# A recurrent attention block with an MLP on one core: LoRA's products ahead, loads in another order, weight halves and one conv tap on ScalarE

## The chip, the cores and the metric

The kernel runs on one core of a Trainium2 chip. The metric is the device time of one execution in microseconds. The core has TensorE (PE, with its weight loads as PEld), VectorE (DVE), ScalarE (ACT), GpSimd (POOL) and SyncE (SP), each with an instruction queue of its own that is worked off in order. Engines wait for each other by semaphores. A "bank" is one of eight PSUM banks of 128 x 512 fp32.

## The reference

The input is x, 8 sequences of 512 tokens of width 128. Per sequence:

```
xn = layernorm(x)
z, xBC, dt = split(xn @ in_proj_w.T)            # 256, 384, 4 columns
dt = softplus(dt + dt_bias)
xBC = silu(conv_b + sum_k shift(xBC, k) * conv_w[:, k])      # 4 taps, causal
x_ssm, B, C = split(xBC)                        # 256, 64, 64; B and C are 32 complex numbers
theta = clip(theta_base + tanh(xn @ theta_w1) @ theta_w2, -pi/2, pi/2)      # LoRA, 4 heads x 32
log_z = complex(-(lambda_base + eta * theta**2) * dt, theta * dt)
state_t = exp(log_z_t) * state_{t-1} + B_t * (x_ssm_t * dt_t)      # per head, 64 x 32 complex
y_t = real(C_t . state_t) + D * x_ssm_t
g = rmsnorm(y * silu(z)) * norm_w
attention = g @ out_proj_w.T
h = 2*relu(s0 * [xn, -xn] @ (+-1)); h = 2*relu(s1 * h @ (+-1)); mlp = s2 * h @ (+-1)      # 512, 512, 128
out = x + attention + mlp
```

## The kernel before

One sequence is one turn of a software pipeline. Turn n holds the front of sequence n (theta, phases, decays, the MLP), the back of sequence n-1 (the products that give y, the gate, the output projection) and the first projections of sequence n+1. There is a prologue (weights made ready, first projections), a first turn without a back, six middle turns, a turn without a successor, and a drain that holds the last back alone. A general version follows for inputs whose exponents are large; a flag skips it, and it does not run here.

The order of the work on each engine is written out by hand: `pipelined(n, ...)` in each engine's block and `first_turn` on DVE and ACT. An instruction deep in one queue can hold up all behind it. The names that the change touches:

- **High and low halves.** fp32 values are multiplied as a high and a low fp16 half. For xn, `xn_t` makes xh on ACT and `xn_low` makes xl on DVE (L521). For weights, `pair` makes both on DVE (L923, L924) during the prologue. For the MLP, `mlp_high` makes h0h and h1h on ACT (L1132), `h0_low` and `h1_low` make h0l and h1l on DVE (L784); four tiles each.
- **Phases and decays (DVE).** `thetas` clips; `phases` multiplies theta with dt spread over the partitions in bank 2 (`ph`, L580), scans (L581), removes whole turns and leaves the fraction (L599). `exponents` multiplies rates with dt into `lz` in bank 2 (L607), scans it into SBUF (L613) and clamps it there (L614). ACT makes sine and cosine (`trig`, L1097 to L1100) and the growth factors by exp into bank 3 (`decays`, L1106 and L1114), with a table load ahead of the first exp. `decayed(n, 0)`, `(n, 1)` and `(n, 2)` multiply K, Q and U by them (L657), real and imaginary part in two instructions each.
- **B and C.** `bc_products` (PE, L1424) fills bank 2. `bc_taps` sums four taps on DVE: the newest one (L564), then three more (L567). `silu_bc` (ACT, L1071) and 16 DMAs on SP repeat the rows. POOL rotates C by the phases, waits for msq and makes `rms` (L1253), multiplies B with the rotated C (U, L1272 to L1277), and then makes B times K (L1302 to L1307, signal `s_bk`), which the products "across the middle" (PE, L1493) need.
- **LoRA.** `lora1` (PE, L1398) writes bank 3 and waits for the decay of U, which reads it; `tanh_lora` on ACT; `lora2` (PE, L1438) writes banks 3 and 1; `theta_input` on ACT (L1086). `dt_spread` (PE, L1445) transposes dt into bank 2 once the taps have been read.
- **The back.** PE makes G (L1483), across (L1493); DVE masks four heads (`g_base`, L715); PE transposes K (L1503), makes y within a chunk (L1513, L1520), the states (L1529), which DVE adds up (`states`, L751, L753), and y from the states (L1549). DVE gates (L775), ACT squares, PE projects (`out_products`, L1573) and sums squares (L1564), DVE makes msq (L780), POOL rms, DVE writes the output (`final`, L797). `add_mlp` (DVE, L788) frees bank 4, for which the next turn's G products wait.
- **Loads.** `first_loads` are issued on SP behind x of sequence 0 and all constants, `loads` on ACT's queue. Each list has one semaphore, so a reader waits for its last load. DVE waits for all constants before the first layernorm, and for all of `first_loads` before the first scaling of weights (L920); ACT waits for all of `loads` before anything else.

## Time and profile before

| | us |
|---|---|
| median of 3 runs (353.70, 353.71, 354.59) | 353.71 |
| the profiled execution's own time | 354.44 |
| its span | 352.6 |
| PE busy | 297.9 (84%) |
| DVE busy | 282.9 (80%) |
| ACT busy | 172.3 (49%) |
| POOL busy | 181.6 (52%) |

The span runs from the first to the last instruction of the profiled execution. Busy shares are means over stages with different limits. A turn is read best from one start of the G products (PE, L1483) to the next. In the views, a bracket behind a row tells how long its engine had stood idle and what released it.

### The profile page before, as it was taken

To read this page: it belongs to the slowest core of one execution; us is meant where nothing else is said; L and a number is where in the kernel's file an instruction comes from. 1 tells how busy PE (TensorE), PEld (TensorE's weight loads), DVE (VectorE), ACT (ScalarE), POOL (GpSimd) and SP (SyncE) were. 2 spreads that over 40 slices of the span, in tenths; PEclk is the share of its full clock that TensorE was granted. 3 is DMA by queue.
4 is the path that set the end of the run, shared out by engine and by line. 5 is a ranking of instruction groups with operands and counts; after the bars stand their busy time and mean duration, and the time that the engine had idled before them with its cause. 6 is when DMAs were issued, how large, how long until landed. Compare 5 with 4: busy or idle time off the path is not lost.

```text
span 352.6 us, 9459 instructions
## 1 busy us (share of the span) xinstructions
PE 297.9 (84%) x3927; PEld 209.6 (59%) x3927; DVE 282.9 (80%) x694; ACT 172.3 (49%) x313; POOL 181.6 (52%) x157
## 2 busy tenths in 40 slices
PE   0467649998999999999999999989998999986690
PEld 0344115677667765776677657775677667753580
DVE  2598898989888988888888898888889887879521
ACT  0404663467545763377437744774467543671110
POOL 0100156205894389718990889168944894194101
PEclk9969586999999999999999999999999999999996
DMA  6400310032002301140113110221013010301001
GB/s 167 104 1 2 92 28 0 3 90 64 6 26 61 90 4 31 41 100 15 33 33 81 42 32 14 73 68 31 2 48 77 0 33 19 95 11 31 2 4 35
DMA packets 19163, 14.85 MB, mean 42 GB/s; under 512 B 5062, under 2 KB 14891, under 8 KB 19115
## 3 DMA queue, kind: packets, MB, share of 16 engines
q1 hardware_dynamic: 16090, 13.67, 15.1%
q10 hardware_dynamic: 3024, 0.52, 0.9%
q8 instruction: 32, 0.52, 0.7%
q14 instruction: 17, 0.13, 0.1%
HBM read 3.70 MB, written 2.10 MB: 16 GB/s over the span
## 4 chain that ended last, share of the span: by engine, by line
DVE 34%; PE 32%; POOL 16%; ACT 8%; issue 6%; DMA 2%; SPq 1%; POOLq 0%; DVEq 0%
POOL btmp L1272 6%; PE bank L1483 5%; POOL btmp L1273 4%; PE bank L1549 4%; PE bank L1564 3%; PE bank L1473 3%; DVE gT L775 3%; PE bank L1431 3%; DVE phl L581 3%; PE bank L1493 3%; DVE cum L613 2%; POOL Ure L1277 2%; POOL Uim L1277 2%; ACT z L1080 2%; POOL rms L1253 2%
## 5 line engine op out<-in xcount | busy, mean ns | idle before, releaser
L1272 POOL TENSOR_TENSOR btmp<-cres,Xre 128x512 f32<-128x512 f32 x8 | 10.7, 1341 | 84.2 <-ACT Xre L1100 84.2
L1464 PE MATMUL bank<-h0h,W 128*128 128x512 f16 x128 | 49.8, 389 | 4.4 <-DVE h1l L784 2.6
L1414 PE MATMUL bank<-XW,xh 128*128 128x256 f16 x256 | 51.6, 289 | 0.0
L1465 PE MATMUL bank<-h0l,W 128*128 128x512 f16 x128 | 49.5, 387 | 0.0
L1414 PE MATMUL bank<-XW,xl 128*128 128x256 f16 x128 | 36.8, 288 | 0.0
L1414 PEld LDWEIGHTS bank<-XW,xh 128*128 128x128 f16 x256 | 26.3, 103 | 8.0 <-issue 0.9
L1132 ACT ACTIVATE h1h<-bank 128x512 f16<-128x512 f32 x32 | 18.1, 589 | 24.9 <-PE bank L1465 24.9
L1464 PEld LDWEIGHTS bank<-h0h,W 128*128 128x128 f16 x128 | 12.8, 100 | 24.0 <-DVE h0l L784 7.2
L784 DVE SCALAR_TENSOR_TENSOR h0l<-bank,h0h 128x512 f16<-128x512 f32 x32 | 21.9, 687 | 6.4 <-ACT h0h L1132 6.2
L784 DVE SCALAR_TENSOR_TENSOR h1l<-bank,h1h 128x512 f16<-128x512 f32 x32 | 22.0, 687 | 5.5 <-ACT h1h L1132 5.2
L1247 POOL TENSOR_TENSOR rstd<-vare,minus_half 128x4 f32<-128x4 f32 x8 | 8.3, 1041 | 34.9 <-DVE negmean L516 34.5
L1132 ACT ACTIVATE h0h<-bank 128x512 f16<-128x512 f32 x32 | 18.2, 592 | 13.5 <-PE bank L1454 13.3
L715 DVE TENSOR_TENSOR GT<-bank,const 128x512 f32<-128x512 f32 x32 | 19.9, 682 | 5.1 <-PE bank L1493 5.1
L1253 POOL TENSOR_TENSOR rms<-msq,minus_half 128x4 f32<-128x4 f32 x8 | 8.2, 1019 | 25.0 <-DVE msq L780 25.0
L1465 PEld LDWEIGHTS bank<-h0l,W 128*128 128x128 f16 x128 | 12.8, 100 | 13.6 <-issue 1.1
L1513 PE MATMUL bank<-GT,xd 128*64 128x128 f32 x256 | 20.2, 279 | 0.0
L1520 PE MATMUL bank<-skip_eye,x 128*64 128x128 f32 x256 | 19.4, 273 | 0.0
L567 DVE SCALAR_TENSOR_TENSOR bcsum<-bank,cw,bcsum 128x511 f32<-128x511 f32 (+2 forms) x24 | 18.0, 748 | 0.8
L1473 PE MATMUL bank<-W,h1h 128*128 128x128 f16 x128 | 15.2, 220 | 3.7 <-DVE h1l L784 3.7
L1573 PEld LDWEIGHTS bank<-OW,gT 128*128 128x128 f32 x128 | 14.9, 191 | 3.9 <-DVE gT L775 3.9
L1573 PE MATMUL bank<-OW,gT 128*128 128x128 f32 x128 | 16.4, 281 | 0.9 <-DVE gT L775 0.9
L1564 PEld LDWEIGHTS bank<-const,gsq 128*128 128x128 f32 x128 | 15.5, 192 | 1.0
(211 smaller groups left out, 890.8 us busy)
## 6 DMA issues: line engine op xcount, KB each, us to landing
xtok<-in_x SPq DMA_DIRECT2D x8, 256.0 KB, 3.2
cres<-bc SPq DMA_DIRECT2D x32, 64.0 KB, 2.1
cims<-bc SPq DMA_DIRECT2D x32, 64.0 KB, 2.1
bres<-bc SPq DMA_DIRECT2D x32, 64.0 KB, 2.1
bims<-bc SPq DMA_DIRECT2D x32, 64.0 KB, 2.1
out<-osb SPq DMA_DIRECT2D x8, 256.0 KB, 2.3
const<-constants SPq DMA_DIRECT2D x1, 576.0 KB, 5.6
KT<-in_in_proj_w SPq DMA_DIRECT2D x1, 320.0 KB
```

The lines of the kernel that those rows point to most:

```text
L715: V.tensor_tensor(GT[:, h, :, :], gbanks[fast][h][:].rearrange("p (c t) -> p c t", t=CH), view(const, 0, 128, mask, [[0, NCH], [1, CH]]), ...
L784: V.scalar_tensor_tensor(lo[:, f, :], bank[4 + f % 2][:], 0.0, high[:, f, :], ALU.max, ALU.subtract).then_inc(sig.sem, 1)
L1132: step(sig, A.activation(hi[:, f, :], bank[4 + f % 2][:], ACT.Relu))
L1272: P.tensor_tensor(btmp[0][:], a[:], f1, ALU.mult).then_inc(sig.sem, 1)
L1414: last = M.matmul(dst, tok(x, c, k), w[:, k, :], start=False, stop=(k == TAPS - 1 and q == 2))
L1464: M.matmul(bank[4 + f % 2][:], w, h0h[:, k, :], start=(k == 0), stop=False)
L1465: last = M.matmul(bank[4 + f % 2][:], w, h0l[:, k, :], start=False, stop=(k == MT - 1))
L1473: last = M.matmul(bank[4][:, D * c:D * c + D], h[:, k, CH * c:CH * c + CH], W2[:, k, :], start=(k == 0 and r == 0), stop=(k == MT - 1 and ...
L1513: last = M.matmul(y_part(h, CH * c, CH), xd[:, c, HEAD * h:HEAD * h + HEAD], GT[:, h, c, :], start=(c == 0), stop=True, skip_group_check=True)
L1520: last = M.matmul(y_part(h, CH * c, CH), x2s[p][:, c, HEAD * h:HEAD * h + HEAD], skip_eye[:, h, :], start=False, stop=True, skip_group_che ...
L1564: last = M.matmul(sums_in[:, c:c + 1], gsq[:, half, CH * c:CH * c + CH], all_ones(1), start=(half == 0), stop=(half == 1))
L1573: last = M.matmul(out_in[:, D * c:D * c + D], gT[:, h, CH * c:CH * c + CH], OW[:, h, :], start=(h == 0), stop=(h == 1))
```

## The change

In the prologue:

- Loads are sorted by need into six groups with semaphores of their own. ACT's queue issues the in-projection and the conv weights, then the small rows; SP's issues x, the identity alone (a ninth of the constants), the rows of dt and the output projection, the MLP's weights, the rest of the constants, then late columns.
- PE starts transposing when the first tap is scaled, instead of when all are.
- The high halves of the transposed weights, and W1, W2, OW and `skip_eye`, are made on ACT. DVE makes the low halves, now behind the rows' preparations and signs. ACT makes the high halves of BCW and ZW once DVE has done all taps' low halves.
- PE does dt, bc and LoRA's first products before those of x; DVE sums the taps of sequence 0 and makes its dt while x's products run.

In the turns:

- The newest tap moves from DVE to ACT (`newest_tap`). The three others of sequence n+1 are summed at the end of turn n.
- `lora1(n+1)` comes before `mlp_out(n)`, `bc_products(n+1)` in the middle of MLP 1, `lora2(n)` first in the turn (banks 3 and 2), `dt_spread(n)` behind the G products, and z's products behind those across the middle.
- On DVE the layernorm of the next sequence opens the turn; the masks come between `ph` and its scan; the states come ahead of the last phase step; h0's second low half comes right behind the first, with both ahead of the scan of exponents; the decay of K comes after all four.
- The rates go to bank 3 and are scanned in place there; the clamp reads PSUM. The turn's next transposes of xn wait for the rates, no longer for the scan.
- `decayed` is one instruction of 1024 elements per pair. `largest` runs once at the end, over one column per sequence.
- On ACT, theta's input comes before `silu_bc` and `silu_z`, and `decays(n, True, 0)` behind h0's third and fourth high half (in the first turn behind xn's high half).
- The sums of squares are split: half of them come behind the first tile of MLP 1.

```diff
-            v.wait_ge(tables, 16)
+            setup(V.memset(minus_one[:], -1.0))
             layernorm(0, 0, 16)
-            v.wait_ge(first_weights, 16 * len(first_loads))
+            v.wait_ge(in_proj_in, 16 * len(in_proj_loads))
...
+            v.wait_ge(rows_in, 16 * len(row_loads))
             pair(CB[0:1, :], CB[BLK:BLK + 1, :], cb_row[:], BIAS_SCALE)
...
+            for k in range(TAPS):
+                low(XW[0][:, k, :], XW[1][:, k, :], tap_bank[k][:, 0:INNER], k + 1)
...
+            low(DTW[0][:], DTW[1][:], bank[5][:, 0:HEADS], TAPS + 1)
+            low(BCW[0][:], BCW[1][:], tap_bank[0][:, INNER:INNER + 128], TAPS + 2)
             xn_low(0)
```

```diff
             # DVE, a middle turn
-                if has_front:
-                    bc_taps(n)
-                if has_back:
-                    for h in EMPTIED:
-                        g_base(n - 1, True, h)
+                if has_next:
+                    early_layernorm(n + 1)
                 if has_front:
                     thetas(n)
-                    phases(n)
-                if has_back:
-                    states(n - 1)
-                if has_front:
+                    phases(n, new_states, masks)
                     exponents(n, True, gates)
...
                     h1_low(n, 2)
+                    h1_low(n, 3)
                     decayed(n, 2)
-                    h1_low(n, 3)
-                    largest(n)
-                    early_layernorm(n + 2)
+                if has_next:
+                    bc_taps(n + 1)
                     add_mlp(n, n % XBUFS)
```

```diff
             # exponents
-                step(V.tensor_tensor(lz[:], nl[:], bank[2][:], ALU.mult), linked=False)
+                rates = growth if fast else lz
+                step(V.tensor_tensor(rates[:], nl[:], bank[2][:], ALU.mult), linked=False)
...
-                    step(V.tensor_tensor_scan(cum3[:, 1, :], all_ones(T), lz[:], 0.0, ALU.mult, ALU.add))
-                    step(V.tensor_scalar(cum3[:, 0, :], cum3[:, 1, :], SAFE, -SAFE, ALU.min, ALU.max), by=2)
+                    step(V.tensor_tensor_scan(growth[:], all_ones(T), growth[:], 0.0, ALU.mult, ALU.add))
+                    step(V.tensor_scalar(cum3[:, 0, :], growth[:], SAFE, -SAFE, ALU.min, ALU.max), by=2)
```

```diff
             # ACT, a middle turn
+            def newest_tap(n):
+                act.wait_ge(t_bc.sem, t_bc.done(n))
+                step(a_tap, A.activation(bcsum[:], bank[2][:], ACT.Copy, scale=cw[:, 2, PAD:TAPS]))
...
+                    theta_input(n)
                     silu_bc(n, True)
                     silu_z(n, p)
-                    theta_input(n)
...
+                    mlp_high(a_h0, t_h0, h0h, n, (2, 3))
                     decays(n, True, 0)
-                    mlp_high(a_h0, t_h0, h0h, n, (2, 3))
```

```diff
             # PE, a middle turn
-                    lora1(n, True)
+                    lora2(n)
...
+                if has_front:
+                    dt_spread(n)
...
-                    z_products(n)
-                    dt_spread(n)
+                    z_products(n)
...
-                    lora2(n)
...
-                    mlp1(n, (0, 1))
+                    mlp1(n, (0,))
+                if has_back:
+                    sums_of_squares(b, (2, 3))
+                if has_front:
+                    mlp1(n, (1,))
                     if has_next:
                         dt_products(n + 1)
                         x_products(n + 1, 1)
+                        bc_products(n + 1)
                     mlp1(n, (2, 3))
                     if has_next:
                         x_products(n + 1, 0)
+                        lora1(n + 1, True)
                     mlp_out(n)
-                    if has_next:
-                        bc_products(n + 1)
```

## Rows read from the trace of the kernel before

**Rows 1.** Windows of two turns: length, busy time and instructions of each engine, granted clock.

```profile
144.20:181.47 37.27, 35.64 (x492) 25.54 (x490) 32.06 (x78) 21.33 (x39) 24.89 (x22) 1.00 0.17 44
293.30:327.25 33.95, 27.69 (x415) 19.33 (x413) 29.83 (x55) 16.64 (x30) 17.18 (x15) 1.00 0.16 41
```

**Rows 2.** Timeline of PE, one middle turn: start, us, engine, line, op, idle before.

```profile
146.29 0.34 PE L1493 MATMUL bank<-Qre,Bre 32*64 32x64 f32 x8
...
148.69 0.60 PE L1445 MATMUL bank<-const,dtb 128*128 128x128 f32 x4
...
156.04 0.45 PE L1549 MATMUL bank<-Qre,S 32*64 32x128 f32 x8 [0.70 <-DVE S L751]
...
157.51 0.39 PE L1453 MATMUL bank<-xh,W 128*128 128x512 f16 x1
...
161.83 1.84 PE L1564 MATMUL bank<-const,gsq 128*128 128x1 f32 x16
...
163.96 0.38 PE L1464 MATMUL bank<-h0h,W 128*128 128x512 f16 x1
...
178.48 0.23 PE L1473 MATMUL bank<-W,h1h 128*128 128x128 f16 x1 [0.36 <-DVE h1l L784]
```

**Rows 3.** Timeline of DVE, the same turn.

```profile
143.93 0.75 DVE L564 TENSOR_SCALAR bcsum<-bank,cw 128x512 f32<-128x512 f32 x1
144.72 2.32 DVE L567 SCALAR_TENSOR_TENSOR bcsum<-bank,cw,bcsum 128x511 f32<-128x511 f32 x3
147.55 2.48 DVE L715 TENSOR_TENSOR GT<-bank,const 128x512 f32<-128x512 f32 x4 [0.52 <-PE bank L1493]
...
155.70 0.28 DVE L751 COPY S<-bank 128x128 f32<-128x128 f32 x1
...
160.89 0.97 DVE L614 TENSOR_SCALAR cum<-cum 128x512 f32<-128x512 f32 x1
...
165.99 0.69 DVE L521 SCALAR_TENSOR_TENSOR xl<-bank,xh 128x512 f16<-128x512 f32 x1
...
176.53 0.69 DVE L657 TENSOR_TENSOR Ure<-Ure,bank 128x512 f32<-128x512 f32 x1 [0.55 <-POOL Uim L1277]
177.14 0.68 DVE L657 TENSOR_TENSOR Uim<-Uim,bank 128x512 f32<-128x512 f32 x1
...
180.48 0.75 DVE L788 SCALAR_TENSOR_TENSOR o<-bank,sffn,xtok 128x512 f32<-128x512 f32 x1 [0.34 <-PE bank L1473]
```

**Rows 4.** Timelines of ACT and POOL, the same turn.

```profile
158.15 1.09 ACT L1132 ACTIVATE h0h<-bank 128x512 f16<-128x512 f32 x2 [0.57 <-PE bank L1454]
...
160.29 1.28 ACT L1106 ACT_TABLE_LOAD   x1
161.89 0.60 ACT L1106 ACTIVATE bank<-cum 128x512 f32<-128x512 f32 x1 [0.31 <-DVE cum L614]
...
166.89 1.02 POOL L1253 TENSOR_TENSOR rms<-msq,minus_half 128x4 f32<-128x4 f32 x1 [1.34 <-DVE msq L780]
...
175.23 1.27 POOL L1277 TENSOR_TENSOR Uim<-btmp 128x512 f32<-128x512 f32 x1
```

**Rows 5.** Timeline of DVE, first turn.

```profile
37.09 0.69 DVE L580 SCALAR_TENSOR_TENSOR ph<-theta,bank 128x512 f32<-128x512 f32 x1
...
45.94 0.43 DVE L614 TENSOR_SCALAR cum<-cum 128x512 f32<-128x512 f32 x1
```

**Rows 6.** Chain that ended last, from 0 to 70: start, us, what.

```profile
4.13 5.99 DMA tw<-in_theta_w
...
20.02 0.60 DVE xl L521
...
53.70 2.67 PE bank L1414 x12
...
69.75 0.37 PE bank L1483
```

**Rows 7.** DMA view of the first 16 us: packets, then one issue, its median to landing.

```profile
DMA packets 6107, 2.39 MB, mean 149 GB/s; under 512 B 2806, under 2 KB 5979, under 8 KB 6107
...
lam<-in_lambda_base ACTq DMA_DIRECT2D x1, 0.5 KB, 6.8
```

More of the change, by code:

```diff
@@ L560, in bc_taps @@
                 step = chain(s_conv, n)
-                if not (isinstance(n, int) and n == 0):
-                    v.wait_ge(a_bc.sem, a_bc.at(n, 0))
-                v.wait_ge(t_bc.sem, t_bc.done(n))
-                step(V.tensor_scalar(bcsum[:], bank[2][:], cw[:, 2, PAD:TAPS], None, ALU.mult))
+                v.wait_ge(a_tap.sem, a_tap.done(n))
                 for k in range(PAD - 1, -1, -1):
@@ L579, in phases @@
                 v.wait_ge(t_dtr.sem, t_dtr.done(n))
-                step(V.scalar_tensor_tensor(ph[:], theta[:], 1.0 / (2 * math.pi), bank[2][:], ALU.mult, ALU.mult))
+                step(V.scalar_tensor_tensor(ph[:], theta[:], 1.0 / (2 * math.pi), bank[2][:], ALU.mult, ALU.mult), linked=False)
+                if ahead_of_scan:
+                    ahead_of_scan()
+                step.link()
                 step(V.tensor_tensor_scan(phl[:], c_("restart"), ph[:], 0.0, ALU.mult, ALU.add), linked=False)
@@ L655, in decayed @@
                     v.wait_ge(s_v.sem, s_v.done(n))
-                for dst, src in (((Kre, pcs), (Kim, psn)), ((Qre, Rre[:]), (Qim, Rim[:])), ((Ure, Ure[:]), (Uim, Uim[:])))[part][halves[0]:halves[-1] + 1]:
-                    step(V.tensor_tensor(dst[:], src, growth[:], ALU.mult), linked=False)
+                dst, pitch, src = ((K, 2 * T, X), (Q, T, R), (U, T, U))[part]
+                first, count = halves[0], len(halves)
+                step(V.tensor_tensor(dst[:, first:first + count, :], view(src, 0, 128, pitch * first, [[pitch, count], [1, T]]),
+                                     view(growth, 0, 128, 0, [[0, count], [1, T]]), ALU.mult), linked=False, by=count)
             def other_half(step, dst, first, second, op, shape):
@@ L928, in _ @@
                 setup(V.memset(TW1[k][:, LORA:], 0.0), False)
[L929 to L938 removed]
+            pair(TW1[0][:, 0:LORA], TW1[1][:, 0:LORA], tw1[:], WSCALE)
             setup(V.tensor_scalar(sign[:], s012[:], 0.0, None, ALU.is_gt))
@@ L957, in _ @@
-            for h in range(2):
-                setup(V.tensor_scalar(OW[:, h, :], bank[4][:, 256 + 128 * h:384 + 128 * h], normw[:, h:h + 1], None, ALU.mult))
-            for h in range(HEADS):
-                setup(V.tensor_scalar(skip_eye[:, h, :], ident, skip[:, h:h + 1], None, ALU.mult))
             assert nd[0] == SETUP, nd
-            v.wait_ge(set_dve, SETUP)
-            dt_input(0)
+            v.wait_ge(tables, 16)
+            bc_taps(0)
             dt_steps(0)
@@ L1118, in decays @@
                     act.wait_ge(a_exp.sem, a_exp.at(n, 3))
-                    step(a_exp, A.activation(sq[:], sq[:], ACT.Relu, bias=spread[:, 0:1], accum_out=beyond[:]))
+                    step(a_exp, A.activation(sq[:], sq[:], ACT.Relu, bias=spread[:, 0:1], accum_out=beyond[:, n:n + 1]))
                 else:
@@ L1435, in lora2 @@
                 pe.wait_ge(a_tanh.sem, a_tanh.done(n))
-                for part, into in enumerate((bank[3][:, 0:T // 2], bank[1][:, T // 2:])):
+                pe.wait_ge(s_conv.sem, s_conv.done(n))
+                for part, into in enumerate((bank[3][:, 0:T // 2], bank[2][:, T // 2:])):
                     rows = slice(HALF * part, HALF * part + LORA)
```

287 lines of the change are left out of this document (167 added, 120 removed).

## The prediction

> **What bounds the kernel now.** I read the windows by turn first, then the timelines of one middle turn engine by engine, then the chain of the prologue. A turn starts where TensorE starts the G products of the sequence behind. The first such start is at 69.75 [rows 6]; six middle turns follow, 37.27 us each; the turn without a successor takes 33.95, from 293.30 to 327.25, and the drain the rest of the span, 25.35 [rows 1]. In a middle turn no engine is full: PE 35.64, DVE 32.06, POOL 24.89, ACT 21.33 of 37.27. So the period is a loop of waits. I write t for the time since 144.20, the turn's start.
>
> The loop as the rows give it. Masks start 1.26 after the products across the middle (t 3.35) [rows 2, 3]. TensorE goes through y and waits for the states (156.04, with 0.70 idle). The high half of an MLP tile starts 0.64 after its first matmul (157.51 to 158.15) [rows 2, 4]. The next sequence's low half, xl, ends at t 22.48, msq is made beside it, and rms starts on POOL at t 22.69. POOL then works without a pause until U's imaginary part ends at t 32.30 [rows 3, 4]. From there: decay of U 1.2, last h1 low half 0.6, MLP output 1.8, bc and LoRA products 1.2, next turn at 37.27 (4.97 after U). Two chains end nearly together: POOL's, and TensorE's own work. TensorE's gaps between issues, added along its timeline (the longest two ahead of 156.04 and 178.48 [rows 2]), are 2.3, so its work is 34.9.
>
> The prologue is 69.7 us. Its chain begins with a wait of 5.99 for a small load, ends at 10.12, and the first low half xl ends at 20.62 [rows 6].
>
> **The change in a middle turn.** DVE loses the newest tap (0.75, from PSUM; spaced 0.79 with its link) to ACT, which takes it in its idle time, and `largest` (about 0.25). Three pairs of decays become three instructions of double length. Two such products start 0.61 apart and take 0.69 [rows 3], so a merged one is bounded by 1.1 and 1.4 and I take 1.2: no gain. ACT has 16 us of idle time in a turn, so the tap is free there, if it comes at the right time: it runs some 8 us before its reader.
>
> The clamp moves its source from SBUF to PSUM. It took 0.97 beside a working POOL, 0.43 in the first turn with POOL idle [rows 3, 5]; from PSUM the nearest row is the newest tap, 0.75. Bounds 0.43 and 1.0; I take 0.75, a gain of 0.22 for all that is behind it.
>
> Here the Trainium skill has a rule (VectorE: DVE Perf Modes, "Mode 2×_2P — use both read ports for one tensor"): the double rate for one fp32 source is had only from SBUF, since PSUM has one read port. By it alone the move would cost 0.32 against 0.43; beside POOL the trace shows the double rate worth nothing (0.97), so the case goes by the row, and the rule fits the 0.75 of the tap.
>
> Now the turn is walked again. TensorE: G products 2.02, dt spread 0.53, products across at t 2.65, z behind them. DVE: layernorm 1.55 now at the start of the turn, theta (0.43 to 0.97), and `ph`, which waits for the dt spread until 2.8. Masks start at 2.65+1.26 = 3.9, end at 6.4. y products begin when they are done, t 6.8 (before: 6.46). So moving the masks behind the spread costs 0.35 there. But states now come ahead of the last phase step, at 9.7 to 10.5 (before 11.50, 155.70) [rows 3]; TensorE, which arrives at 11.3, no longer waits for them. MLP tiles 0 and 1 start at 12.8 (before 13.31) [rows 2]. The phase step ends at 11.1 (before 11.6), so POOL starts C's rotation 0.45 earlier.
>
> That gain on POOL buys nothing, since rms and behind it U wait for msq. Gates 12.9 to 14.3, both h0 low halves to 15.5, scan 1.3, clamp to 17.5, third h0 low half to 18.2. TensorE's tile 3 starts at 17.4; its high half on ACT runs 18.05 to 18.65. In the old order the exp table came before these tiles: load 160.29, 1.28 long, exp at 161.89 (t 17.69) [rows 4]. In the new order it comes behind them: load 18.65 to 19.95, exp to 20.55. The decay of K, one instruction, 20.6 to 21.8, then xl to 22.4, msq 22.45. Before: 22.48 and 22.45. So the late exp eats the 0.5 us that the front half won.
>
> The tail. TensorE starts MLP 1 at 18.2 (before 19.76 [rows 2]) since half the sums of squares, 0.85, comes behind tile 0. From 18.2: the old stretch to 178.48 was 14.52 with 0.8 idle, so 13.7 of work, plus 0.85 sums, plus 1.2 bc and LoRA: 33.95; MLP output 1.8 and 0.2 until it is seen, `add_mlp` 0.75 [rows 3], G products at 36.75 to 36.9. POOL's chain: msq 22.45, U at 32.3 as before. LoRA's first product waits for U's decay (it writes the bank of the growth factors): 32.3+1.2 = 33.5, then 0.45+1.8+0.2+0.75+0.06 = 36.8. DVE's: decay of U 1.2, three taps 2.32 [rows 3], `add_mlp` 0.75: 36.6. LoRA 2 (0.64) lies under `add_mlp`. Three chains end within 0.3; the period is 36.85, a gain of 0.42. Six turns: -2.5.
>
> Bounds: if K's decay were not held by the late exp, TensorE's path alone would give 36.4 (-0.9); if collisions shift msq by 0.5, 37.4 (+0.1). In sum -5.5 to +1 over six turns. The turn without a successor: exp comes 0.5 earlier there (no transposes), K and the first h1 low half at the old time, DVE's tail to the end loses 0.1: 33.95 stays. Drain: the same order but for split sums, 25.35 stays.
>
> **The change in the prologue.** Landings were issue plus 6 to 7 us for small columns (lam 6.8) [rows 7]; the first 16 us hold 6107 packets [rows 7], and by the timeline of the DMA engines they pass between 2.4 and 12.9, about 580 per us. Now the in-projection goes first on ACT's queue with cw (1024 packets) beside as many on SP's: 2.4 + 2048/580 = 5.9, with about 1 us until seen, 7. The nine small row loads are behind it: about 4100 packets, 9.5 to 10.6; bound above 13.2, when the last small columns now land, below 8. DVE's tap scalings run 7.0 to 8.7, transposes follow pair by pair, all done at 10. High halves on ACT (4 of 0.42) overlap; but DVE waits for the row loads, then has 1.2 of CB and LoRA weights and 1.7 of signs and scales: 13.5. Then four low halves 1.7, the two small ones behind ACT 0.7, xl 0.65: 16.6 against 20.62 [rows 6]. Gain 4.0 (bounds 1.4 and 6.9).
>
> Next, dt, bc and LoRA go ahead of the x products, so taps, dt steps and tanh lie under them. Before, projections ended at 30.6, then taps until 34.3, then spread, LoRA 2, theta, `ph` at 37.09 [rows 5]. After: projections 16.65 to about 26.4 (same matmuls; the first 4 us at 1.2 GHz as before, where one chunk of x takes 2.67 and its bias 0.3 [rows 6], the rest at 2.4 GHz, where a chunk takes 1.6); W1, W2, OW and skip on ACT between 20 and 24.7 (W1 four times a 0.54 row: 2.2), hidden; LoRA 2 to 27.1, theta input behind silu and dt repeat 28.4, spread, `ph` at 29.2. Gain 7.9.
>
> Part of it is given back. In the first turn exp follows xn's high half, which waits for MLP 1's first tiles on TensorE: exp ends 43.7 (48.7 before, gain 5.0). xl comes first, then the rotated part (2.05 as POOL is idle, 4.1 before), K 45.6, Q 47.5, first h1 low half 49.0, B part 51.05, dt and xd 53.5, dt steps 56.1, h1 57.3, U's decay 58.45, then three taps 2.32, new here, B and K 2.05, `add_mlp` 0.75: 63.5. Before 69.7. So the prologue gives -6.2; bounds -9.5 and -2.5, mostly from the row loads (3.0) and the clock during the first turn.
>
> **Sum.** 63.5 + 6 x 36.85 + 33.95 + 25.35 = 343.9 against a span of 352.6: -8.7. The profiled execution took 354.44, 1.84 more than its span; so 345.7. The median of the runs shown, 353.71, is 0.73 below the profiled one: 345.0.
>
> **Rivals.**
> (a) Only the prologue gains; the loop keeps 37.27, because msq stays at its place and across-products, masks and y are 0.35 later. For: POOL's start at msq is unmoved in my own walk. Against: 1.2 us of products leave the stretch behind the MLP output. 345.0+2.5 = 347.5.
> (b) The loop gains 1 us a turn: ACT and POOL take the new order without the late exp (for example tile 3 earlier). For: TensorE's work is 34.9. Against: K's decay can't start before exp. 345.0-3.5 = 341.5.
> (c) Slower than before. The exp that now stands behind h0's high halves delays K, xl, msq, rms and U one for one; from msq at t 24.0 on (1.5 later than my walk), six turns cost 6 x 1.5 = 9, more than the 8.7 won, and at 1.7 later the kernel takes 355. For: the table load lies bare between tile 3 and K. Against: the load took 1.28, and exp followed it without further wait but the clamp's [rows 4].
> The Trainium skill (ScalarE: Activation LUTs, "What ACT_TABLE_LOAD costs") gives a drain of about 1.38 us on top of a load of 1.283; by it msq would move by up to 1.4, six turns by 8.3, and the time would be 353. The trace agrees with the 1.28; no such drain is to be seen there.
> (d) The loads don't come sooner: the row loads land at 13.2, where the last small columns land now. Then 2.6 of the prologue's gain goes: 347.6.
> The Trainium skill (DMA: Bandwidth & Descriptors, "Issuing engines are not separate DMA queues") says that queues of several engines share the same 16 engines, so two queues alone give nothing; only order can. Both queues were in use before.
>
> **Chances.** Forecast (340.5 to 350 as its own range) 0.52; (a) 0.14; (b) 0.12; (d) 0.13; (c) 0.05, nothing gained 0.04. The range 340 to 350.5 leaves out about 0.2. A measurement of this kernel tells 0.3%, 1.1 us, from no change: faster 0.90, same 0.03, slower 0.07.
>
> **What would show it.** In the profile after: the first G products at 63.5; the row loads seen at about 10.5 and xl near 16.6; a period of 36.85; no TensorE idle ahead of the state products; exp's table load behind the fourth h0 high half at t 18.7 and K's decay right after exp; clamp 0.75; `add_mlp` with TensorE waiting after LoRA 2. I am wrong in the step on the loop if the period is under 36.4 or over 37.3, and on the loads if `ph` is not between 27 and 32.

## The result, and the profile after

The changed kernel took 346.34 us (median of 345.85, 345.93, 346.75 and 347.13), the kernel before 353.78 beside it: a ratio of 0.9755, with a 95% interval of 0.9714 to 0.9797. 345.0 was predicted, with a range of 340 to 350.5. The profiled execution of the changed kernel took 345.85 with a span of 344.1, that is 8.5 less than the span of before.

Below are lines of its page: busy time by engine, the granted clock in 40 slices of 8.6 us, and the chain that ended last. Before, that chain was TensorE for a third and POOL for a sixth; now it is TensorE for two thirds and POOL for nothing.

```profile
PE 295.3 (86%) x3927; PEld 208.5 (61%) x3927; DVE 266.5 (77%) x640; ACT 182.6 (53%) x336; POOL 180.5 (52%) x157
PEclk9999889999999999999999999999999999999995
PE 66%; DVE 21%; ACT 6%; issue 3%; DMA 2%; ACTq 1%; POOL 0%; DVEq 0%; POOLq 0%
```

Windows of the changed kernel: the first two are middle turns, then the turn without a successor and the drain. They answer to [rows 1]. Their borders lie 0.07 before the first G product of the turn; by the products themselves the first turn behind the prologue starts at 63.49, the last at 284.52, and the drain lasts from 318.53 to the end, 25.5.

```profile
63.42:100.26 36.84, 35.48 (x489) 25.54 (x489) 30.34 (x74) 20.53 (x38) 23.27 (x21) 1.00 0.17 45
137.10:173.94 36.84, 35.48 (x489) 25.53 (x489) 31.30 (x74) 21.89 (x41) 24.87 (x22) 1.00 0.17 45
284.45:318.46 34.01, 27.08 (x408) 18.85 (x408) 26.46 (x48) 15.72 (x28) 17.46 (x15) 1.00 0.16 40
318.46:344.10 25.64, 14.16 (x327) 12.64 (x327) 8.17 (x22) 2.11 (x4) 1.51 (x2) 0.84 0.05 14
```

Timelines of one middle turn of the changed kernel, PE first; t counts from 137.17. They answer to [rows 2 to 4].

```profile
155.48 0.39 PE L1515 MATMUL bank<-h0h,W 128*128 128x512 f16 x1 [0.53 <-DVE h0l L803]
...
159.75 0.17 PE L1439 MATMUL bank<-DTW,xh 128*128 128x4 f16 x1
...
170.75 0.30 PE L1448 MATMUL bank<-xh,TW 128*64 128x256 f16 x2
...
171.20 0.23 PE L1524 MATMUL bank<-W,h1h 128*128 128x128 f16 x1
...
174.01 1.17 PE L1534 MATMUL bank<-U,K 32*128 32x128 f32 x32 [0.21 <-DVE o L807]
```

```profile
138.34 1.13 DVE L532 TENSOR_SCALAR vare<-mv 128x4 f32<-128x4 f32 x1
...
146.78 0.29 DVE L770 COPY S<-bank 128x128 f32<-128x128 f32 x1 [0.35 <-PE bank L1580]
...
154.00 0.69 DVE L632 TENSOR_SCALAR cum<-bank 128x512 f32<-128x512 f32 x1
...
155.60 1.28 ACT L1129 ACT_TABLE_LOAD   x1
...
156.90 0.60 ACT L1129 ACTIVATE bank<-cum 128x512 f32<-128x512 f32 x1
...
157.63 1.22 DVE L676 TENSOR_TENSOR K<-X,bank 128x1024 f32<-128x1024 f32 x1 [1.32 <-ACT bank L1129]
...
158.77 0.69 DVE L538 SCALAR_TENSOR_TENSOR xl<-bank,xh 128x512 f16<-128x512 f32 x1
159.37 0.15 DVE L799 TENSOR_SCALAR msq<-bank 128x4 f32<-128x4 f32 x1
...
169.38 1.22 DVE L676 TENSOR_TENSOR U<-U,bank 128x1024 f32<-128x1024 f32 x1
```

The table load stands bare between the last h0 high half and exp, and K waits 1.32 for it. The dt products wait, by the program, for xl and for msq, which DVE makes right behind it. xl ends at t 22.29, msq at 22.35, and TensorE takes the dt products at t 22.58, 0.22 behind its last MLP 1 product, as it spaces these products among themselves. From there the trace shows no wait of TensorE until `add_mlp`: 11.45 to the MLP output, 2.81 more to the next turn. On the way LoRA's first product, which must wait for U's decay, starts at t 33.58; U's decay ends at t 33.43.

Prologue, DVE; it answers to [rows 5, 6].

```profile
10.99 0.28 DVE L944 TENSOR_SCALAR CB<-cb_row 1x256 f16<-1x256 f32 x1 [3.00 <-DMA eta<-in_viscosity_eta]
...
13.53 1.41 DVE L950 SCALAR_TENSOR_TENSOR XW<-bank,XW 128x256 f16<-128x256 f32 x4
...
15.49 0.68 DVE L538 SCALAR_TENSOR_TENSOR xl<-bank,xh 128x512 f16<-128x512 f32 x1
...
29.50 0.69 DVE L594 SCALAR_TENSOR_TENSOR ph<-theta,bank 128x512 f32<-128x512 f32 x1 [0.36 <-PE bank L1496]
```

### The profile page after: what moved, and what is told of

Read it like the earlier page. It is cut to its first block, busy times and chain, and to the rows that moved or that the text cites. A ratio compares the mean times of both kernels' runs of the same rounds, so it can differ in the third digit from the quotient of the medians.

```text
span 344.1 us, 9422 instructions
## 1 busy us (share of the span) xinstructions
PE 295.3 (86%) x3927; PEld 208.5 (61%) x3927; DVE 266.5 (77%) x640; ACT 182.6 (53%) x336; POOL 180.5 (52%) x157
## 4 chain that ended last, share of the span: by engine, by line
PE 66%; DVE 21%; ACT 6%; issue 3%; DMA 2%; ACTq 1%; POOL 0%; DVEq 0%; POOLq 0%
PE bank L1464 12%; PE bank L1515 7%; PE bank L1516 7%; PE bank L1534 5%; PE bank L1564 5%; PE bank L1571 4%; PE bank L1524 4%; DVE h0l L803 4%; PE bank L1600 4%; PE bank L1481 3%; DVE gT L794 3%; PE bank L1544 3%; ACT z L1103 3%; PE bank L1615 2%; DVE bank L631 2%
## 5 line engine op out<-in xcount | busy, mean ns | idle before, releaser
L1320 POOL TENSOR_TENSOR btmp<-cres,X 128x512 f32<-128x512 f32 x15 | 19.0, 1270 | 80.0 <-ACT X L1123 79.5
L1516 PE MATMUL bank<-h0l,W 128*128 128x512 f16 x128 | 50.5, 395 | 0.0
L1464 PE MATMUL bank<-XW,xh 128*128 128x256 f16 x256 | 48.7, 278 | 0.0
L1464 PE MATMUL bank<-XW,xl 128*128 128x256 f16 x128 | 35.5, 277 | 0.0
L1103 ACT ACTIVATE z<-bank 128x512 f32<-128x512 f32 x16 | 8.7, 595 | 30.4 <-PE bank L1481 30.4
L1320 POOL TENSOR_TENSOR btmp<-bres,R 128x512 f32<-128x512 f32 x14 | 23.0, 1640 | 0.6
L1301 POOL TENSOR_TENSOR rms<-msq,minus_half 128x4 f32<-128x4 f32 x8 | 8.1, 1018 | 27.4 <-DVE msq L799 27.4
L1325 POOL TENSOR_TENSOR R<-btmp 128x512 f32<-128x512 f32 x15 | 19.0, 1269 | 4.3 <-DVE R L682 3.2
L1325 POOL TENSOR_TENSOR U<-btmp 128x512 f32<-128x512 f32 x14 | 17.7, 1265 | 5.6 <-DVE U L682 4.7
L1534 PE MATMUL bank<-U,K 32*128 32x128 f32 x512 | 16.5, 276 | 4.0 <-DVE o L807 4.0
L794 DVE TENSOR_TENSOR gT<-bank,z 128x256 f32<-128x256 f32 x32 | 11.3, 416 | 11.0 <-PE bank L1600 11.0
```

Source lines behind the costliest of these rows:

```text
L794: step(V.tensor_tensor(gT[:, half, cols], bank[6 + half][:, cols], z2s[p][:, half, cols], ALU.mult), linked=False)
L1103: step(a_silu, A.activation(z2s[p][:, half, :], bank[6 + half][:], ACT.Silu, scale=1 / PS))
L1320: P.tensor_tensor(btmp[0][:], a[:], f1, ALU.mult).then_inc(sig.sem, 1)
L1325: P.tensor_tensor(dst[:], btmp[0][:], btmp[1][:], op).then_inc(sig.sem, 4 if other else 1)
L1464: last = M.matmul(dst, tok(x, c, k), w[:, k, :], start=False, stop=(k == TAPS - 1 and q == 2))
L1516: last = M.matmul(bank[4 + f % 2][:], w, h0l[:, k, :], start=False, stop=(k == MT - 1))
```

## The experiments

Times are medians; "the changed kernel" is 346.34. The runs were made in several sessions; the kernel before, run beside them, had medians of 353.9 to 354.6, so medians that differ by less than 1 say little. Turns are read from the one profiled execution of each run, from first G product to first G product, and t counts from the turn's first G product.

### What sets the period

**e1_exp_first.** On ACT, exp goes back ahead of h0's third and fourth high half.

```diff
+                    decays(n, True, 0)
                     mlp_high(a_h0, t_h0, h0h, n, (2, 3))
-                    decays(n, True, 0)
```

> The changed kernel with one order of ScalarE undone in the middle turns: the growth exp ahead of h0's third and fourth high halves, as in the kernel before. Theory A (TensorE's own path through the start of MLP 1 sets the period): the third high half now waits for the clamp (t 17.6) and exp (18.2), ends at 18.8, its low half at 19.4, MLP 1 starts at 19.5 instead of 18.4, and the period rises by about 1.1 to 37.9; over seven turns the span goes from 344.1 to about 351. Theory B (the late exp holds K, xl, msq and POOL, and that sets the period): msq 0.5 earlier, the period falls to about 36.3, span about 341.

Measured 362.4 (359.1 to 368.7; ratio to before 1.018, 1.009 to 1.027), far outside both. MLP 1 now waits 1.74 for h0's low half and starts 1.2 later. Three of the six middle turns take 38.0 to 38.1, as theory A has it. The others take 39.7, 39.7 and 41.5, and in them the granted clock falls to half right behind that wait. So it does in the turn without a successor, which takes 36.4 instead of 34.0. Windows of e1: an undisturbed turn, a disturbed one, and a stretch of the latter.

```profile
141.45:179.45 38.00, 35.46 (x489) 25.53 (x489) 30.71 (x73) 21.86 (x41) 24.82 (x22) 1.00 0.17 43
179.45:220.95 41.50, 38.87 (x489) 27.04 (x489) 30.13 (x74) 21.96 (x41) 26.07 (x22) 0.92 0.16 40
```

```profile
201.00:205.50 4.50, 4.50 (x16) 2.76 (x15) 2.12 (x4) 2.28 (x5) 1.41 (x2) 0.50 0.00 0
```

So exp behind the high halves, which I had called the step that eats the gain, is itself worth 1.2 us a turn, and up to 3.4 more where the clock falls.

**e2_table_early.** A one-column exp is put in ACT's queue ahead of h0's last two high halves, so that only the table load moves forward.

```diff
                 if has_front:
+                    A.activation(warm[:], minus_one[:], ACT.Exp)
                     mlp_high(a_h0, t_h0, h0h, n, (2, 3))
                     decays(n, True, 0)
```

> The changed kernel with one tiny exp of 128x1 ahead of h0's third high half in the middle turns, so that the table load runs in ScalarE's idle time there and the growth exp follows the fourth high half at once. Theory A (TensorE's path binds): K starts 1.3 earlier, msq about 1.1 earlier, U about 1.1 earlier, and the period stays at 36.85 within 0.1; span 344 within 1. Theory B (what the prediction said of the late exp: it eats what the front half won, and without it TensorE's path alone would give 36.4): period 36.4, span about 341.5.

Measured 348.48. K's decay starts at t 19.06 instead of 20.46, and xl ends 1.4 earlier, as meant. Four of the middle turns still take 37.0, one 37.2. The table load pushes h0's third high half back from t 16.58 to 17.04, so that TensorE waits 0.68 instead of 0.53 ahead of MLP 1, starts it 0.16 later, and comes to the dt products 0.16 later (t 22.74).

```profile
157.01 0.39 PE L1517 MATMUL bank<-h0h,W 128*128 128x512 f16 x1 [0.68 <-DVE h0l L804]
```

Theory B, the prediction's own, falls. Theory A is right in that the period doesn't shrink: K and xl came 1.4 earlier, msq and rms 1.0, U's decay 0.4, and nothing followed. Its span of 344 did not come. The profiled span is 347.3: the first loop turn, at a granted clock of 0.96, takes 38.5, the drain is 1.3 longer, and the other five turns are 1.0 longer together.

**e7_sums_before.** The second half of the sums of squares goes ahead of MLP 1's first tile on TensorE.

```diff
                     mlp0(n, (3,))
-                    mlp1(n, (0,))
                 if has_back:
                     sums_of_squares(b, (2, 3))
                 if has_front:
+                    mlp1(n, (0,))
                     mlp1(n, (1,))
```

> The second half of the sums of squares (0.8 us on TensorE) goes ahead of MLP 1's first tile, into the 0.53 us in which TensorE waits for h0's low half, instead of behind that tile. Theory A (TensorE reaches the dt products too early then: it already waits 0.22 there for xl, which ends at t 22.3; the 0.5 won ahead of MLP 1 is lost again at xl): period 36.7 to 36.85, time 346 +-0.8. Theory B (TensorE's own order sets the period and xl is no bound): period 36.3, first G unchanged, time 343.2.

The median, 349.47 (346.22 to 349.76), says little: the first loop turn took 38.4 at a clock of 0.96. The undisturbed turns decide, and they give 36.83, as theory A had it. TensorE could have taken the dt products at t 22.04; it took them at 22.49, behind xl and msq, with a wait of 0.45.

```profile
161.90 0.16 PE L1439 MATMUL bank<-DTW,xh 128*128 128x4 f16 x1 [0.45 <-DVE msq L799]
...
172.99 0.30 PE L1448 MATMUL bank<-xh,TW 128*64 128x256 f16 x2
```

The wait of 0.22 that the expectation saw in the changed kernel is none; it is the spacing of the products. And a third bound shows here: the dt products come 0.08 earlier than in the changed kernel, LoRA's first product doesn't. It starts at t 33.58 again, 0.15 behind the end of U's decay (t 33.43 in both).

**e13_table_signs_sums.** Both of these, and the edit of e4 (below).

> Three edits: the exp table asked for ahead of h0's third high half (e2, which made K's decay and xl 1.3 us earlier in the turn but TensorE's MLP 1 0.2 later, period 36.95), the preparations of the signs behind xl in the prologue (e4, 343.87), and the second half of the sums ahead of MLP 1 (e7). Theory A (two waits in series hold TensorE at the same place, h0's low half ahead of MLP 1 and xl ahead of the dt products; only both together give way): the sums cover the wait ahead of MLP 1, which then starts at t 18.6, dt products at t 22.0 instead of 22.45; period 36.4, time 341.3. Theory B (another bound stands behind them, U's decay by POOL's chain: rms and with it U come only with msq): POOL's chain also starts with msq, so TensorE would wait ahead of LoRA or the MLP output; period 36.8, time 343.9.

Measured 338.61 (ratio to before 0.957, 0.953 to 0.961), better than theory A's 341.3. MLP 1 starts at t 18.46 without a wait and the dt products at 21.93, where theory A has 18.6 and 22.0. The period is 36.17 where it has 36.4; e4's part is not in it, as e4 alone leaves the turns at 36.84. The rows: two middle turns, then PE and DVE around the dt products of the second (its first G product is at 135.24).

```profile
99.05:135.15 36.10, 35.34 (x489) 25.65 (x489) 30.39 (x73) 21.90 (x42) 24.81 (x22) 1.00 0.18 46
135.15:171.35 36.20, 35.34 (x489) 25.67 (x489) 30.49 (x74) 22.00 (x42) 24.91 (x22) 1.00 0.18 45
```

```profile
153.70 0.39 PE L1523 MATMUL bank<-h0h,W 128*128 128x512 f16 x1
...
155.43 0.69 DVE L542 SCALAR_TENSOR_TENSOR xl<-bank,xh 128x512 f16<-128x512 f32 x1
...
157.17 0.17 PE L1447 MATMUL bank<-DTW,xh 128*128 128x4 f16 x1
```

This settles what bounds the loop. The dt products start when two things are done: xl with msq behind it, and TensorE's own work since h0's low half. In the changed kernel these end within 0.3 of each other (t 22.35 and 22.58). Moving either alone gives nothing; moving both gives 0.67 a turn, 36.17 instead of 36.84. U's decay has to come along, and does, since POOL's chain to it starts with msq: it ends at t 32.21, 1.2 earlier. Where it doesn't bind, in the changed kernel, e1, e2, e10 and e13, the same 11.45 follow from the dt products to the MLP output; in e7 it adds 0.08. What is left for TensorE's waits in the loop is 0.8: it is busy for 35.34 of 36.17.

**e3_lora1_last.** On TensorE, LoRA's first product goes behind the MLP output.

```diff
                         x_products(n + 1, 0)
+                    mlp_out(n)
+                    if has_next:
                         lora1(n + 1, True)
-                    mlp_out(n)
```

> The changed kernel with LoRA's first product behind the MLP output instead of ahead of it, in the middle turns. Theory A (its place matters because tanh lies between LoRA's two products): add_mlp starts 0.45 earlier, but LoRA's second product waits for tanh, about 0.7 bare, so the G products start 0.4 later; period 37.25, span about 347. Theory B (the place is indifferent or costs, since add_mlp is the last wait): the period is 36.85 or falls by up to 0.4, span 341.5 to 344.

Measured 347.35 (346.12 to 352.97; the profiled execution is the longest of the five). Its undisturbed turns take 36.99. The way is theory A's: `add_mlp` starts 0.46 earlier in the turn (t 35.57 instead of 36.03), but LoRA's second product has to wait for tanh.

```profile
137.55 0.70 PE L1489 MATMUL bank<-th,tw 48*128 48x256 f32 x4 [0.48 <-ACT th L1071]
```

The size is not: the wait is 0.48 and not 0.7, and the period is 0.15 longer and not 0.4, between the two theories. LoRA's position is worth 0.15 a turn.

**e9_tap_dve.** The newest tap goes back to DVE.

```diff
-                v.wait_ge(a_tap.sem, a_tap.done(n))
+                if not (isinstance(n, int) and n == 0):
+                    v.wait_ge(a_bc.sem, a_bc.at(n, 0))
+                v.wait_ge(t_bc.sem, t_bc.done(n))
+                step(V.tensor_scalar(bcsum[:], bank[2][:], cw[:, 2, PAD:TAPS], None, ALU.mult))
...
                     dt_exp(n + 1)
-                    newest_tap(n + 1)
```

> Against the changed kernel (346.34) one part is undone: the newest tap goes back to DVE, 0.75 us from PSUM and 0.04 of link, ahead of the three others at the end of the turn. Theory A (DVE's tail was full: U's decay ends at t 33.4, three taps at t 35.66, and add_mlp waits 0.37 for TensorE): four taps end at t 36.45, add_mlp 0.42 later, period 37.26; the first turn's end 0.8 later; time 349.7. Theory B (TensorE is what the turn ends on, and the tap finds room in DVE's idle time): 346.3 to 347.

Measured 351.21. Four of the six middle turns take 37.2 to 37.3, as in theory A: LoRA 2 now waits for the taps and `add_mlp` starts behind them.

```profile
175.70 0.74 DVE L810 SCALAR_TENSOR_TENSOR o<-bank,sffn,xtok 128x512 f32<-128x512 f32 x1
...
175.93 0.70 PE L1488 MATMUL bank<-th,tw 48*128 48x256 f32 x4 [0.60 <-DVE bcsum L584]
```

The tap on ACT is thus worth 0.4 a turn, as much as the loop gained in all. The span, 347.9, is theory A's 349.7 less 1.75, though by another way: the first turn hides its tap (`add_mlp` at 62.5), one loop turn at a clock of 0.96 takes 38.8, and another 37.6 at full clock. The median is 1.5 over theory A because this kernel's profiled execution took 3.1 more than its span, the changed kernel's 1.75. Why is open.

**e12_states_late.** DVE adds up the states behind the last phase step again.

```diff
-                    phases(n, new_states, masks)
+                    phases(n, None, masks)
+                    states(n - 1)
                     exponents(n, True, gates)
```

> Against the changed kernel (346.34) one part is undone: DVE adds up the states behind the last phase step again, instead of ahead of the rounding's subtraction. Theory A (the order is neutral: without the states and the 0.35 of wait ahead of them the phase steps end at about t 10.3, the states at 11.3, and TensorE comes for them at 11.37): period 36.8 to 36.9, time 346.3. Theory B (the move took away the 0.70 us that TensorE waited for the states before, and this is what shortened the loop): TensorE waits 0.3 to 0.7 again, gates, h0's low halves and MLP 1 are late by that, period 37.1 to 37.5, time 348 to 350.5.

Measured 346.06, turns of 36.84. Theory A. The states are added up at t 10.85, and TensorE comes for them at t 11.37, without a wait. So their order against the phase step bought nothing; before, they started at t 11.50. What took away TensorE's wait of 0.70 is then the rest of DVE's new order ahead of them; no run takes that apart.

### The clamp

**e5_clamp_sbuf.** Scan into SBUF, clamp from SBUF.

```diff
-                    step(V.tensor_tensor_scan(growth[:], all_ones(T), growth[:], 0.0, ALU.mult, ALU.add))
-                    step(V.tensor_scalar(cum3[:, 0, :], growth[:], SAFE, -SAFE, ALU.min, ALU.max), by=2)
+                    step(V.tensor_tensor_scan(cum3[:, 1, :], all_ones(T), growth[:], 0.0, ALU.mult, ALU.add))
+                    step(V.tensor_scalar(cum3[:, 0, :], cum3[:, 1, :], SAFE, -SAFE, ALU.min, ALU.max), by=2)
```

> The scan of the rates goes to SBUF again and the clamp reads SBUF, as in the kernel before; all else as in the changed kernel. In the changed kernel the clamp from PSUM took 0.69 us in a middle turn, beside a working POOL, and 0.69 in the first turn, where POOL is idle. Theory A (the lock of the two-port form, as the Trainium skill's page on DVE perf modes has it, and as the 1.13 us of the 128x4 tensor_scalar beside a POOL op suggests against 0.17 elsewhere): the clamp from SBUF takes about 0.43 where POOL is idle and waits for POOL's running op where it works, so 0.9 to 1.6 in a middle turn; h0's third low half and MLP 1 are late by 0.2 to 0.9, and the period goes from 36.84 to 37.0 to 37.7: time 347.5 to 351. Theory B (it is only DVE's own work, and a source in SBUF saves 0.26): the clamp takes 0.43 everywhere, MLP 1 starts 0.26 earlier, period 36.6: 345.

Measured 346.18, turns of 36.83: no difference. The rows of the clamp are worth more: first turn with POOL's operation, then a middle turn with POOL's.

```profile
39.08 1.26 POOL L1320 TENSOR_TENSOR btmp<-cres,X 128x512 f32<-128x512 f32 x1 [12.12 <-ACT X L1123]
...
39.10 1.52 DVE L632 TENSOR_SCALAR cum<-cum 128x512 f32<-128x512 f32 x1
...
153.90 0.43 DVE L632 TENSOR_SCALAR cum<-cum 128x512 f32<-128x512 f32 x1
...
154.10 1.35 POOL L1320 TENSOR_TENSOR btmp<-cres,X 128x512 f32<-128x512 f32 x1
```

Where POOL had begun 0.02 before, the clamp took 1.52; where it meets the seam between two of POOL's operations, 0.43, and POOL's next one takes 1.35 instead of 1.27. From PSUM it took 0.69 in both places (39.06 and 154.00 in the changed kernel). So a clamp from SBUF waits for POOL's running operation. It ended 0.28 behind that operation (40.62 and 40.34), and so it did in the kernel before, where it took 0.97 from 160.89 [rows 3]:

```profile
160.31 1.27 POOL L1277 TENSOR_TENSOR Rre<-btmp 128x512 f32<-128x512 f32 x1
```

The Trainium skill (SBUF — State Buffer, "SBUF: two separate sides") says that DVE in a two-port mode and GpSimd share a port pair under an exclusive lock that the first one keeps for its whole instruction; the times agree. The expectation put the lock on the Trainium skill's page on DVE perf modes; it stands on this one. Theory A had the mechanism right and its place wrong: here it strikes only once, in the first turn. In a middle turn theory B's 0.43 holds, and MLP 1 does start 0.28 earlier, as it said. But the dt products gain only 0.08 of that, since they wait for xl and msq, and LoRA's first product, behind U's decay, starts at t 33.58 as before. This is e7's finding a second time.

### The prologue

**e4_signs_late.** The eleven preparations of signs and scales go behind xl, and their loads (s0 to s2, dt_bias, lambda, eta) get a semaphore of their own.

```diff
             v.wait_ge(rows_in, 16 * len(row_loads))
             pair(CB[0:1, :], CB[BLK:BLK + 1, :], cb_row[:], BIAS_SCALE)
...
-            setup(V.tensor_scalar(sign[:], s012[:], 0.0, None, ALU.is_gt))
...
             xn_low(0)
+            v.wait_ge(signs_in, 16 * len(sign_loads))
+            setup(V.tensor_scalar(sign[:], s012[:], 0.0, None, ALU.is_gt))
...
```

> The changed kernel with a smaller first group of row loads (theta_w1 and the conv bias row alone); the scales s, dt's bias, lambda and eta get a semaphore of their own, and DVE makes signs and scales behind xl instead of ahead of the weights' low halves. Theory A (the row loads and the 1.4 us of small preparations gate xl, and xl gates all until the first turn's end): rows seen at about 8, low halves right behind ScalarE's high ones from 11.4, xl ends at about 14.2 instead of 16.2, the first G products at 61.5 instead of 63.5, span 342.1. Theory B (the first G products are set by something else, such as ScalarE's preparations or the clock of TensorE): xl earlier, first G products within 0.5 of 63.5.

Measured 343.87 (ratio to before 0.971, 0.965 to 0.976). The span is the expected 342.1, but its parts are not. DVE doesn't wait for rows at all any more (CB at 7.57); what it then waits for is the first high half on ACT, 2.33. xl ends at 13.75, 2.4 earlier; 0.3 of that is chance, as x itself landed that much earlier in this execution (first layernorm at 4.53, not 4.86). The first G product starts at 59.95, 3.5 earlier, which is more than xl gained; the granted clock from 24 to there was 0.95 instead of 0.91. 1.3 is given back in the drain: from the last `add_mlp` to the end 27.7 instead of 26.4, at a clock of 0.82 instead of 0.85. So what lands late is one or more of the six columns spread over partitions, not the rows that the weights need: these were there by 7.57.

**e8_highs_dve.** The high halves of x's weights are made on DVE again, beside their low halves.

```diff
             for k in range(TAPS):
-                low(XW[0][:, k, :], XW[1][:, k, :], tap_bank[k][:, 0:INNER], k + 1)
+                pair(XW[0][:, k, :], XW[1][:, k, :], tap_bank[k][:, 0:INNER], WSCALE)
...
-            for k in range(TAPS):
-                high(XW[0][:, k, :], tap_bank[k][:, 0:INNER])
```

> Against the changed kernel (346.34) one part of the prologue is undone: the high halves of the transposed in-projection weights for x (4 of 128x256) are made on DVE again, ahead of their low halves. Theory A (DVE is the chain there: busy without a pause from 10.99 to 16.2): 4 more instructions of about 0.3 and a link between the two of a pair, xl ends 1.3 to 1.6 later and so does the first G product: 347.8. Theory B (they find room while DVE waits 3.0 us for the small rows; no, as they stand behind that wait in its queue, but the projections have slack): under 347.

Measured 348.22, first G product 1.25 later (64.74). Theory A, though xl itself is 2.2 later (pairs are 0.79 apart, lone low halves 0.33; and the rows landed 0.4 later). The span is 3.1 longer than the changed kernel's; the other 1.9 are in the drain, 27.4 instead of 25.5, so that theory A's 347.8 is met in part by a drain that it didn't foresee.

### The clock

**e10_exp_first_sums.** e1 with e7's order on TensorE.

> Two edits: exp ahead of h0's third and fourth high half (as in e1_exp_first, which took 362.4), and the second half of the sums ahead of MLP 1's first tile. In e1 TensorE waited 1.74 us ahead of MLP 1 in every turn; two turns had a period of 38.05, and four had one of 39.7 to 41.5, with a granted clock of 0.5 for 3.3 to 7 us right behind that wait. The sums fill 0.85 of the wait. Theory A (it is the length of TensorE's pause after which the clock falls): pause 0.9, no fall behind it in the middle turns; all six at 37.9 to 38.05, time 353 to 355. Theory B (the clock falls for another reason, the later exp or a state of the chip): periods of 39.7 to 41.5 again in half of the turns, time 359 or more.

Measured 351.66; six of the seven executions lie between 350.93 and 353.2, one took 370.24, at a mean clock of 0.85. The wait ahead of MLP 1 is 0.96, and four middle turns take 37.2 to 37.35 at full clock, 0.7 less than theory A expected: I had left out that the sums then no longer stand between MLP 1's first tile and the dt products. But the two other turns (40.4, the first, and 38.8) do show a fall at the end of this shorter wait; in the first there is another one behind the 1.80 that TensorE waits ahead of its G products.

```profile
272.68 0.61 PE L1515 MATMUL bank<-h0h,W 128*128 128x512 f16 x1 [0.96 <-DVE h0l L803]
```

```profile
272.50:275.80 3.30, 3.12 (x8) 1.16 (x9) 3.25 (x6) 1.69 (x4) 2.09 (x3) 0.50 0.00 0
```

So the falls are rarer and cost less (1.5 to 1.6 behind this wait, against 1.7 to 3.4), but theory A's "no fall" is not so, and theory B's times are not met either. The length of the pause alone doesn't decide.

**e14_filled_first_turn.** e13 with products that nobody reads in TensorE's pauses of the first turn.

```diff
+            def idle_products(count):
+                for k in range(count):
+                    M.matmul(bank[0][:], W0[:, 0:128], W0[:], start=True, stop=True)
```

> e13 (338.61) plus 39 products in TensorE's queue whose result is read by nobody (W0 by W0, 128x512, 0.21 us apart), in the six places of the first turn where TensorE waited 0.5 to 1.8 us: 7 and 6 in MLP 0, 7 ahead of the dt products, 4 ahead of MLP 1's third tile, 7 ahead of LoRA, 8 ahead of the first G products. In e13 the granted clock fell to 0.5 behind these waits: from 31 to 37, from 41 to 45 and from 61.5 to 65.4; the turn behind the first G products took 37.80 against 36.15 for the next ones. Theory A (a pause of TensorE of 1.2 us or more brings the fall, as in e1 and e10): the clock stays at 1.0 there; 1.6 less in the turn behind the first G, and about 2.2 less ahead of it, where TensorE's MLP 1 tiles at half clock lie on the path: 334.8 (bounds 334 and 337, as a product too many costs 0.2 at each place). Theory B (the clock falls for another reason, or what it costs is covered by DVE's chain): 338 to 339.5.

The clock did what theory A says in the first turn and the one behind it; the time is theory B's. Windows of e13, then of e14: from t 24 to the first G product or beyond, and the first loop turn.

```profile
24.00:61.25 37.25, 27.06 (x165) 14.15 (x163) 28.88 (x55) 21.63 (x41) 11.74 (x11) 0.86 0.12 29
...
61.25:99.05 37.80, 36.93 (x489) 27.12 (x489) 30.29 (x73) 20.68 (x39) 24.07 (x21) 0.95 0.17 44
```

```profile
24.00:61.90 37.90, 33.89 (x270) 18.84 (x271) 30.94 (x66) 22.19 (x41) 12.66 (x12) 1.00 0.13 31
...
61.90:98.00 36.10, 35.26 (x497) 25.58 (x493) 30.18 (x72) 22.00 (x41) 24.84 (x21) 1.00 0.18 46
```

The loop turn gained the 1.6 that were expected (36.18 against 37.77), the stretch ahead of it 1.0 and not 2.2 (first G product at 60.31). So the last `add_mlp` came 2.6 earlier (309.9 against 312.5). The span gained only 1.3, because the drain took 27.8 from there instead of 26.5, with a clock of 0.82 instead of 0.86. Why the clock falls more in the drain of some runs is open. The median is 339.44 (336.81 to 339.6) against e13's 338.61 (337.47 to 340.85): no difference that these runs can tell. Pauses of 1.30 and 1.74 were left in e14 (they end at 26.7 and 46.0), and the clock stayed at 1.0 behind them; one of 1.74 was followed by half clock in some turns of e1 and not in others. The 1.80 ahead of the first loop turn is in the changed kernel, e4, e5, e8 and e12 too, and no fall follows there. In the loop turns of these traces every fall comes at the end of a pause or right behind it, but the pause alone doesn't decide.

The version that beats both kernels is e13: 338.61, 4.3% under the kernel before and some 2.2% under the changed one (338.61/346.34; two different sessions, so that ratio has no interval of its own).

## Why the prediction was right, step by step

- **The sum.** First G product 63.5 predicted, 63.49 measured; turns 36.85 and 36.84; the turn without a successor 33.95 and 34.01; drain 25.35 and 25.5. Right. The medians differ by 7.4, not 8.6, since the profiled execution of the changed kernel is the quickest of its four and that of before is 0.7 over its median.
- **Loads and weights.** Rows expected at 10.5, seen at 10.99; xl expected to end at 16.6, ended at 16.17; `ph` expected at 29.2, came at 29.50. What the step didn't know is which of the small loads are late: e4 shows that the rows for the weights were there by 7.6, and that DVE's wait to 10.99 was for the others.
- **First turn, and the clock in it.** Right, and not in the sum alone: exp ended at 43.79 (43.7 predicted), K's decay at 45.91 (45.6), the dt steps at 56.05 (56.1), U's decay at 58.49 (58.45). What the walk has no term for, though its bounds name it, is the granted clock: from 24 to the first G product it was 0.80 before and is 0.91 now. How much of the gain over the kernel before is the clock's no run tells; e14 puts a price of 1.0 on what e13, at 0.86, had of it ahead of the first G product.

```profile
24.00:69.75 45.75, 35.21 (x213) 19.06 (x211) 40.81 (x108) 22.69 (x41) 14.69 (x12) 0.80 0.10 24
```

```profile
24.00:63.50 39.50, 29.20 (x193) 15.96 (x191) 30.18 (x66) 23.61 (x43) 12.36 (x11) 0.91 0.11 28
```

- **Masks and states.** No wait of TensorE ahead of the states' products, as predicted; but putting the states ahead of the last phase step, which the prediction gives as the reason, had no part in it (e12).
- **The late exp.** K right behind exp, xl and msq at the old place (t 22.3 against 22.5): right. The sentence "if K's decay were not held by the late exp, TensorE's path alone would give 36.4" is wrong. With K freed (e2) the period is 37.0; it takes the sums moved too, and then it is 36.17 (e13). The prediction has MLP 1 start at t 18.2 (measured 18.31) and gives the split sums as the reason. In the trace it starts right behind h0's third low half, after a wait of 0.53. The prediction has that low half end at t 18.2 too, so the start is no luck, but it never names the wait, and so took all of this path for TensorE's own work.
- **The tail.** "Three chains end within 0.3" holds, or nearly. TensorE runs from the dt products to the MLP output without a pause; it sets the end. POOL's chain is just met: U's decay ends at t 33.43, and LoRA's first product, for which 33.5 was predicted, starts at 33.58, no later than TensorE's own work has it. As soon as the dt products come 0.08 earlier (e5, e7), U's decay holds that product at 33.58. In e2 and e13, where U's decay ends 0.4 and 1.2 earlier, it has slack. DVE's chain has 0.37 of slack, its wait ahead of `add_mlp`, and sets the end with one tap more (e9).
- **The clamp.** 0.75 predicted, 0.69 measured, within the bounds of 0.43 and 1.0; 0.97 before was in part a wait for POOL (e5), and the 0.28 won is in the shadow of xl and msq. The merged decay, 1.2 in the prediction, took 1.22.
- **Rivals.** (a) and (b) fall by the period; (d) by the rows at 10.99. (c), the slower one, falls by msq, which ends at t 22.35 and not at 24.0, and by the table load: 1.28 and then exp within 0.02. The drain of 1.38 that the Trainium skill (ScalarE: Activation LUTs, "What ACT_TABLE_LOAD costs") names doesn't show: behind all 17 table loads in the changed kernel's trace the next activation starts within 0.02. e1 shows that the opposite order is the slow one.

## What to carry to other kernels

Where two waits end at nearly the same time at one point, neither shows a gain when it is moved alone: look for the point where the chains meet, and move both. Look for the next point too: a chain that isn't seen to wait may be only just met. Read an experiment's undisturbed turns before its median; e7's turns differ from the changed kernel's by 0.01, its median by 3.1, through the clock. A longer pause on a nearly full TensorE can cost more than its length, and work that must be done anyway is the thing to put into it.

## What the runs showed of the hardware that was not expected

- A 128x4 `tensor_scalar` (L532) took 0.17 with POOL idle and 1.13 in the loop, where it starts 0.16 after a POOL operation of 1.27. The layernorm at the turn's start therefore costs DVE about 1 us more than its instructions. In e13, where it falls nearer to the end of POOL's operation, it takes 0.38, and in e1 and e2, where it starts just behind it, 0.17.
- The granted clock fell to 0.50 for 3.4 to 6.8 us at the end of waits of 0.96 to 1.8 us on TensorE or right behind them, in turns in which TensorE idles for under 3 us in all. It did so in three of the six middle turns of e1 and two of the six of e10, though the wait ahead of MLP 1 was there in all.
